# A clear of a small tile ahead of 346 more row moves of GpSimd in a graph network on one core

## What is computed

```python
x = _layernorm(x + _L0_gnn_ref(x, edge_weight, edge_attr_3, edge_index, ...), axis=-1)
x = _layernorm(x + _L1_gnn_ref(x, edge_index), axis=-1)
x = _layernorm(x + _L2_gnn_ref(x, edge_index, edge_attr_32, ...), axis=-1)
x = _layernorm(x + _L3_gnn_ref(x, edge_attr3_2x32, src, dst, ...), axis=-1)
```

## Time and profile before

| | us |
|---|---|
| median of 3 timed runs | 2048.66 |
| lowest and highest | 2029.43, 2053.27 |
| the profiled execution by the same clock | 2061.06 |
| its span, first to last instruction | 2059.3 |
| VectorE busy | 1345.8 (65%) |
| GpSimd busy | 1284.9 (62%) |
| TensorE busy | 796.0 (39%) |
| ScalarE busy | 486.9 (24%) |

### The profile page before, as it was taken

The page is one execution under the profiler, slowest core; times in us unless marked ns, Lnnn a source line. Parts: engine busy times, 40 slices in busy tenths (PEclk is TensorE's granted clock), DMA queues, the critical chain, the costliest instruction groups (busy, mean ns, idle before and its releaser), DMA issues.

```text
span 2059.3 us, 14157 instructions
## 1 busy us (share of the span) xinstructions
PE 796.0 (39%) x3676; PEld 595.5 (29%) x3676; DVE 1345.8 (65%) x2600; ACT 486.9 (24%) x1014; POOL 1284.9 (62%) x1393
## 2 busy tenths in 40 slices
PE   7801545541333003616313500155621757265122
PEld 3300222220111003515313400145521657265112
DVE  9942959896958970784605496167684899397610
ACT  7721311110100121423202320033320334143200
POOL 8875576674478857515871207888128888637775
PEclk9955866786765555866756755566765776565555
DMA  8072511110110211222201412000000111010000
GB/s 313 16 240 89 201 26 29 27 30 15 20 17 12 76 43 32 100 77 87 89 6 68 158 74 98 4 8 19 18 29 12 32 28 29 18 28 22 10 12 8
DMA packets 64092, 114.25 MB, mean 55 GB/s; under 512 B 27599, under 2 KB 48648, under 8 KB 63224
## 3 DMA queue, kind: packets, MB, share of 16 engines
q1 hardware_dynamic: 24304, 80.96, 10.9%
q0 software_dynamic: 33728, 12.79, 4.5%
q10 hardware_dynamic: 5960, 19.43, 2.5%
HBM read 61.66 MB, written 55.21 MB: 57 GB/s over the span
## 4 chain that ended last, share of the span: by engine, by line
DVE 36%; issue 21%; POOL 20%; PE 12%; another core or an unknown queue 6%; ACT 4%; DMA 1%; DVEq 0%; ACTq 0%; POOLq 0%; PEld 0%; PEldq 0%
DVE work L1484 12%; POOL A_dst L742 8%; POOL work L742 7%; DVE work L1495 5%; PE bank L1261 4%; PE bank L1235 3%; POOL nodes_w L740 2%; POOL A_msg L742 2%; PE bank L1348 2%; DVE A_dst L1484 2%; DVE A_tmp L1484 1%; DVE r L1495 1%; DVE small L1495 1%; PE bank L1421 1%
## 5 line engine op out<-in xcount | busy, mean ns | idle before, releaser
L1495 DVE TENSOR_REDUCE work<-work 128x80 f32<-128x1280 f32 (+3 forms) x147 | 204.5, 1420 | 186.8 <-ACT work L1016 148.9
L742 POOL DMA_INDIRECT A_dst<-in_x,dst_i x196 | 223.4, 1140 | 108.7 <-DVE work L1495 48.7
L1310 PE MATMUL bank<-w2fold,work 128*128 128x384 f32 x392 | 200.6, 658 | 232.4 <-DVE work L1484 136.4
L880 POOL DMA_INDIRECT out<-A_dst,out_i x196 | 211.5, 1079 | 99.0 <-issue 61.7
L1484 DVE TENSOR_TENSOR work<-bank,work 128x384 f32<-128x384 f32 (+1 forms) x294 | 154.6, 589 | 80.3 <-remote 43.1
L1348 PE MATMUL bank<-nodes_w,small 128*128 128x128 f32 (+1 forms) x784 | 137.1, 341 | 162.0 <-ACT small L1006 95.6
L742 POOL DMA_INDIRECT A_src<-x_pos,A_tmp x140 | 145.0, 1036 | 73.1 <-issue 41.8
L1310 PEld LDWEIGHTS bank<-w2fold,work 128*128 128x128 f32 x392 | 91.0, 251 | 340.8 <-issue 310.0
L740 POOL MEMSET nodes_w<- 128x256 f32 x224 | 73.0, 326 | 168.4 <-DMA table<-A_dst 168.2
L1348 PEld LDWEIGHTS bank<-nodes_w,small 128*128 128x128 f32 (+1 forms) x784 | 125.9, 249 | 172.9 <-ACT small L1006 104.6
L742 POOL DMA_INDIRECT work<-table,pos_i x112 | 142.0, 1268 | 30.9 <-POOL nodes_w L740 30.9
(11 more groups left out here) (397 smaller groups left out, 2306.8 us busy)
## 6 DMA issues: line engine op xcount, KB each, us to landing
work<-in_x SPq DMA_DIRECT2D x26, 960.0 KB
x_pos<-A_sum SPq DMA_DIRECT2D x13, 990.0 KB
out<-work ACTq DMA_DIRECT2D x13, 960.0 KB
A_tmp<-ew_turned_rows ACTq DMA_DIRECT2D x49, 130.0 KB
table<-A_dst SPq DMA_DIRECT2D x2, 3136.0 KB
edge_sums<-A_dst SPq DMA_DIRECT2D x2, 3136.0 KB
table<-A_dst SPq DMA_DIRECT2D x13, 448.0 KB
A_tmp<-in_edge_attr_2x SPq DMA_DIRECT2D x49, 112.0 KB
```

The lines of the kernel that those rows point to most:

```text
L742: pool.indirect_dma_start(out=column(t), out_offset=None, in_=of, in_offset=bass.IndirectOffsetOnAxis(ap=idx[:, t:t + 1], axis=0), bounds_ ...
L880: pool.indirect_dma_start(out=out, out_offset=bass.IndirectOffsetOnAxis(ap=out_i[:, t:t + 1], axis=0), in_=A_dst[:, t, :], in_offset=None, ...
L1310: last = nc.tensor.matmul(banks[2 * (u % PAIRS_DEEP) + j][:, 0:PATHS], hid_rows[:, u % PAIRS_DEEP, j * P:(j + 1) * P], w2_rows[:], start=T ...
L1495: return v.tensor_reduce(out=o, in_=a, axis=AX, op=op)
```

## The change

The clear with its wait becomes a function `pause(tile)`, and it is put ahead of these moves too, always on `gtmp[0:HF]`: the 56 gathers of `pos_x`; the moves of `short_columns` (60 takes and 60 stores); the first 22 columns of each call of `second_columns` (3 x 22); and the first four pieces of the result rows (`i < 4`: 20 + 28 + 28 + 28 = 104). That is 346 clears more; the 84 on `gtmp` and the 224 on `nodes_w` stay. No move, no data and no other engine's program is changed.

```diff
@@ -730,15 +730,19 @@
 
             node_limit, edge_limit = pool.to_reg(N_NODES - 1), pool.to_reg(E_PAD - 1)
 
+            def pause(tile):
+
+                issued["cleared"] += 1
+                pool.memset(tile, 0.0).then_inc(cleared, 1)
+                pool.wait_ge(cleared, issued["cleared"])
+
             def gather(column, of, idx, limit, done, columns=range(T), keep=None, cleared_tile=None):
 
                 for t in columns:
                     if keep:
                         keep()
                     if cleared_tile is not None:
-                        issued["cleared"] += 1
-                        pool.memset(cleared_tile, 0.0).then_inc(cleared, 1)
-                        pool.wait_ge(cleared, issued["cleared"])
+                        pause(cleared_tile)
                     pool.indirect_dma_start(
                         out=column(t), out_offset=None, in_=of,
                         in_offset=bass.IndirectOffsetOnAxis(ap=idx[:, t:t + 1], axis=0),
@@ -775,7 +779,7 @@
             gather_dst(range(DST_FIRST * GATHER_CHUNK), keep_to_histogram)
             pool.wait_ge(pos_stored, 32)
             gather(lambda t: pos_x[:, t:t + 1], pos_table, src_i, node_limit, lambda t: pos_rows, range(plain),
-                   keep=keep_to_radial)
+                   keep=keep_to_radial, cleared_tile=gtmp[0:HF])
 
             for k in range(XP_SLOTS):
                 pool.wait_ge(x_stored[k], 16 * len(range(k, D_CHUNKS + 1, XP_SLOTS)))
@@ -795,6 +799,7 @@
                 for t in columns:
                     if keep and keep(t):
                         pool.wait_ge(n_out, keep(t))
+                    pause(gtmp[0:HF])
                     move(t).then_inc(done, 16)
                 if columns.stop < FEWEST:
                     return
@@ -877,6 +883,8 @@
             for i, c in enumerate(LAST_ORDER):
                 pool.wait_ge(final_ready, i + 1)
                 for t in range(T)[c] if isinstance(c, slice) else range(c * GATHER_CHUNK, (c + 1) * GATHER_CHUNK):
+                    if i < 4:
+                        pause(gtmp[0:HF])
                     pool.indirect_dma_start(
                         out=out, out_offset=bass.IndirectOffsetOnAxis(ap=out_i[:, t:t + 1], axis=0),
                         in_=A_dst[:, t, :], in_offset=None, bounds_check=node_limit,
```

## The result

The changed kernel took **1916.43 us** (median; 1913.79 to 1918.39) against 2048.18 us for the kernel before, measured beside it: ratio 0.937, 95% interval 0.931 to 0.943. I had forecast 2053.5 us. It is 132 us faster, by an edit that only adds 346 small clears to GpSimd. Two later sessions (a session is a set of kernels measured together, the kernel before among them) gave 0.937 and 0.933 again. But the experiments also found two sessions in which the kernel *before* ran in 1806 and 1803 us; in the first of them each half of the change made it about 1% slower. Times are medians of all runs, while ratios leave out the few runs over 1.5% above the fastest of their kernel, so a ratio can differ a little from the quotient of two medians.

What follows compares the result with a forecast made beforehand. The chain was read as spread over every engine, VectorE 36% and GpSimd 20%. Six terms of zero plus 4.8 us on GpSimd's last chain, added to the median 2048.66, gave 2053.5 us; range 2030 to 2080.

Steps and rivals of the forecast that it cites:

- The price of a clear, 0.167 us: Every added GpSimd clear: 0.472 us of clear and idle instead of 0.305; 57.8 us of GpSimd time for 346 clears.
- The held-move rival: Cleared GpSimd moves themselves last longer, price 0.442 us each; 24.3 us more in all, 2073 us; chance 0.14.
- the 13.85 us of the earlier trace: One GpSimd move, otherwise 1.00 us, lasted this long across VectorE's 14.85 us of scans with two SBUF inputs.
- costs nothing because it lies in a wait: Clears at pos_x, hop takes and stores, and early result rows fit inside GpSimd's existing waits or slack: zero for each.
- VectorE at 906.0, 1006.3 and 1113.9: Node stage: times in us when VectorE first needs three groups of hop takes; GpSimd, though delayed, would finish before each.
- The terms that I had put at zero: Node stage, first and second hop: added clears hidden before VectorE or GpSimd's next release, the tightest place with 1.9 us left.
- the waits are not slack: GpSimd's waits move along with its moves, so all clears are on the path: 57.8 us, 2106 us; chance 0.07.
- The faster rival: Spaced moves let large transfers through sooner, returning a third of 124 us of unknown-queue waits: 41 us, 2008 us; chance 0.05.
- The crawl: TensorE's slow unused second message pass ends after GpSimd's last move and hides the added clears: no change, 2049 us; chance 0.16.
- The last piece's 4.8 us: Result rows: the fourth piece's 28 clears, 4.7 us, plus 0.1 us spill push GpSimd's last move from 2041.5 to 2046.3.

Runs made afterwards that it cites:

- each half of the change: Kernel before plus only the 186 clears at takes and hops, or only the 160 at pos_x and result rows: 1825.47 and 1828.96 us against 1805.7.
- seven raises: Changed kernel with each clear of gtmp replaced by GpSimd's queue raising the semaphore and waiting for it seven times: 1945.5 us, ratio 0.953, late session.
- with ten in an on-time one: Changed kernel with ten semaphore raises and waits by GpSimd's queue in place of each clear of gtmp: 1799.55 us against 1802.9, ratio 0.998.

## Why the prediction was wrong, step by step

- **The price of a clear, 0.167 us: right.** 430 clears of 166 ns in the median, 0.27 us idle behind them. The held-move rival (a cleared move is itself longer) falls: the 60 takes are longer in the changed kernel (1.25 us in the mean, 15.1 us above 1.00 each in all, against 6.5 before), but with seven raises and no clear in a late session they are nearly as long (14.3 us), and with ten in an on-time one longer still (17.8 us). The Trainium skill (GPSIMD Engine Reference, section 8, Key points) says that GpSimd contends with VectorE instructions of two SBUF inputs. No clear shows it here: the longest of the changed kernel's 430 took 286 ns, so a hold like the 13.85 us of the earlier trace rows is still seen in moves alone.
- **The failing step: "costs nothing because it lies in a wait".** Each sum took the wait as fixed and asked whether GpSimd's delay fits in. Its far end, VectorE at 906.0, 1006.3 and 1113.9, was read as VectorE's own pace. It was not: VectorE's four first waits in the stage took 156.2 us, and 105.6 of them went away when GpSimd's moves were spaced and TensorE's signals came sooner. The terms that I had put at zero for the takes and stores of the hops measured -104.3 us in the node stage. I weighed this in the rival "the waits are not slack" and dismissed it with "VectorE waited for ScalarE and unseen queues there, not for GpSimd". The rows were right. The reading stopped a step early: ScalarE's copies ended on "remote", TensorE's matmuls stood on "issue" for 22 us, and GpSimd's row of moves ended in the same 0.4 us. I had also looked for that tie only with the sign that would make the kernel slower.
- **The faster rival: right rows, wrong mechanism, wrong size.** I took the 124 us of "another core or an unknown queue" for large transfers waiting behind small ones, thought a third of it could come back, and gave 0.05, because a move becomes only one part in eight rarer. No run ties the gain to large transfers, and the density on the engine isn't the measure: seven raises leave it at 1.30 us and gain 98 us. That the right direction stood among the rivals is luck as far as its reason goes.
- **The crawl**: "may even hang on the moves" was right and is shown by the clears on the last 92 moves. I noted it for 17 us at the end, and didn't ask where else in the kernel the same picture stands. That was the clue in hand.
- **The last piece's 4.8 us: small, as said, and not what decides.** From the first instruction of the fourth piece to the end of the last move it was 166.9 us before and 167.7 after (169.2 in the first repeat). But that stretch now starts 141 us sooner.

## What to carry to other kernels

A wait that ends on "remote", "issue" or an unknown queue is not slack until its end is explained: look at what every *other* engine stops or starts doing in the same half microsecond, here one that only issues transfers. Before an edit is costed at nothing inside a wait, ask whether the wait itself depends on the edited engine, in both directions. And where the same kernel takes 1806 us in one session and 2045 in another, a tuning like this one may help the second at the cost of the first: time it in both before it is kept. Count the events in each trace too, and time the kernel once with no recording at all if you can: no run here tells whether this gain would be left then.

## What the hardware showed that I had not expected

- TensorE's signals arrived up to 38.8 us behind the recorded ends of its matmuls, while 95% of those of ScalarE and VectorE stood within 12 ns. The Trainium skill (TensorE: Matmul & The Clock Gate, "The cost: per-tile semaphore tail") gives a tail for matmuls packed as tiles that grows by 26.3 ns with each increment. No run here measures that tail; the 14 ns or so of the on-time sessions are an event behind a modelled end, and the late ones are over a hundred times longer than either.
- The lateness went with how closely indirect transfers are handed to GpSimd, and with the session: 243 us between 1806 and 2049 for one and the same kernel. The record gives chip 14 both to a late session (2043.0 us) and, some ten minutes later, to an on-time one (1802.9 us). If the number means one chip, the condition isn't the chip's alone. Whether it belongs to a host, a time or the recording isn't settled.
- The delay outlasts the moves: 12 of the 36 late signals before come up to 9.3 us after the last move of a row.
- Before 270 us none of the kernel before's 109 signals is over 1 us late; 83 of them fall in the first 90 us, where moves start 1.66 us apart. The trace loses few landing events in the first 100 us (1069 on record, 1383 in an on-time trace) and most in the next 100 (189 against 1834), where only some 20 TensorE signals fall.
